# A two-layer transformer kernel: how attention scores are laid out and ordered on TensorE

## The reference, cut to what matters

```
# layer 0: causal attention inside a batch
dots = einsum('bhid,bhjd->bhij', q, k) * dh**-0.5;  dots = where(causal, -inf, dots)
out  = einsum('bhij,bhjd->bhid', softmax(dots), v)           # then top-1 of 8 experts, silu
# layer 1: self attention (no mask), then the same queries' "recursive" attention on 2 past states
attn = softmax(q @ k.T * SCALE); output = (attn @ v) @ Wo + bo
rattn = softmax(rq @ rk[p].T * SCALE) for p in (0, 1);  rctx = mean over p of rattn @ rv[p]
gate = sigmoid([output, rctx] @ Wg + bg); output = output*(1-gate) + rctx*gate   # then top-2 of 8 experts
```

## Time and profile before

| | |
|---|---|
| median of 3 runs | 1064.85 us |
| the profiled execution's own time | 1054.27 us |
| its span | 1052.3 us |
| TensorE matmul busy | 960.2 us, 91% |
| TensorE weight load busy | 639.5 us, 61% |
| VectorE busy | 788.7 us, 75% |
| ScalarE busy | 591.6 us, 56% |
| GpSimd busy | 228.7 us, 22% |
| mean granted TensorE clock | 0.956 of full |

### The profile page before, as it was taken

The page is one execution under the profiler, slowest core; times in us unless marked ns, Lnnn a source line. Parts: engine busy times, 40 slices in busy tenths (PEclk is TensorE's granted clock), DMA queues, the critical chain, the costliest instruction groups (busy, mean ns, idle before and its releaser), DMA issues.

```text
span 1052.3 us, 17558 instructions
## 1 busy us (share of the span) xinstructions
PE 960.2 (91%) x5970; PEld 639.5 (61%) x5970; DVE 788.7 (75%) x2196; ACT 591.6 (56%) x1270; POOL 228.7 (22%) x360
## 2 busy tenths in 40 slices
PE   8889998888878989999999999999899887999992
PEld 7555665555668645555555555555555442999992
DVE  6888888776465698778888788978878784686673
ACT  2466565454555445767677676775567656443330
POOL 6132323263213234000000100001032112120073
PEclk8899999898989989999999999999999989999996
DMA  4334310010112111110000000000070000212132
GB/s 124 91 99 138 91 51 21 11 50 12 36 37 75 29 28 31 31 41 2 1 11 21 11 1 2 21 14 8 1 260 21 1 3 29 74 44 61 34 86 68
DMA packets 56497, 46.50 MB, mean 44 GB/s; under 512 B 6742, under 2 KB 46038, under 8 KB 56408
## 3 DMA queue, kind: packets, MB, share of 16 engines
q1 hardware_dynamic: 41960, 33.77, 11.4%
q0 software_dynamic: 3072, 6.30, 2.1%
q10 hardware_dynamic: 11376, 5.32, 1.8%
HBM read 22.55 MB, written 14.16 MB: 35 GB/s over the span
## 4 chain that ended last, share of the span: by engine, by line
PE 66%; DVE 20%; POOL 5%; issue 4%; ACT 2%; DMA 2%; DVEq 1%; SPq 0%; POOLq 0%; ACTq 0%
PE st L1346 13%; PE pv L1368 13%; PE ring L1332 12%; PE ring L1249 7%; PE ring L1469 4%; DVE ring L1653 4%; PE st L1456 3%; PE ring L1260 2%; PE ring L1299 2%; DVE M L1649 2%; PE st L1462 2%; DVE M L1656 2%; PE pv L1462 2%; POOL G L1041 1%; PE pv L1279 1%
## 5 line engine op out<-in xcount | busy, mean ns | idle before, releaser
L1123 ACT ACTIVATE Et<-st 128x512 f32<-128x512 f32 (+3 forms) x768 | 380.9, 548 | 211.9 <-PE st L1346 208.2
L1332 PE MATMUL ring<-Kbd,Qa 128*128 128x512 f32 (+3 forms) x512 | 203.3, 417 | 17.4 <-DVE M L1653 7.7
L1346 PE MATMUL st<-Qb,Kbd 128*128 128x512 f32 (+3 forms) x512 | 196.4, 399 | 4.4 <-ACT Et L1123 4.3
L1656 DVE TENSOR_REDUCE M<-ring 128x1 f32<-128x512 f32 x256 | 163.8, 683 | 38.4 <-PE ring L1332 37.0
L1649 DVE TENSOR_REDUCE M<-ring 128x2 f32<-128x512 f32 x256 | 162.9, 683 | 28.6 <-PE ring L1332 27.8
L1346 PEld LDWEIGHTS st<-Qb,Kbd 128*128 128x128 f32 x512 | 96.9, 195 | 89.6 <-ACT Et L1123 65.5
L1332 PEld LDWEIGHTS ring<-Kbd,Qa 128*128 128x128 f32 x512 | 100.6, 200 | 61.8 <-DVE M L1656 19.7
L1653 DVE CUSTOM_DVE_ANT_0 ring<-ring,maskw 128x128 f32<-128x128 f32 (+3 forms) x256 | 120.7, 510 | 20.9 <-PE ring L1332 19.5
L1368 PE MATMUL pv<-Et,Va 128*32 128x512 f32 (+3 forms) x1024 | 120.9, 533 | 0.7 <-POOL Et L984 0.7
L1332 PE MATMUL ring<-RKbd,Qa 128*128 128x512 f32 x256 | 108.2, 430 | 7.0 <-DVE M L1649 6.3
L1346 PE MATMUL st<-Qb,RKbd 128*128 128x512 f32 x256 | 105.4, 427 | 1.2 <-ACT Et L1123 1.0
(11 more groups left out here) (222 smaller groups left out, 1263.6 us busy)
## 6 DMA issues: line engine op xcount, KB each, us to landing
Kbd<-Ksb SPq DMA_DIRECT2D x116, 64.0 KB, 2.0
Yd<-Yt ACTq DMA_DIRECT2D x76, 64.0 KB, 1.5
Xs<-Xd SPq DMA_DIRECT2D x16, 256.0 KB, 3.0
L1W<-in_L1W SPq DMA_DIRECT2D x2, 2048.0 KB, 11.8
Xd<-zero SPq DMA_DIRECT2D x6, 512.0 KB, 3.5
W<-in_L0W SPq DMA_DIRECT2D x8, 258.0 KB, 3.5
W<-in_L0W SPq DMA_DIRECT2D x8, 256.0 KB, 4.2
Xd<-zero SPq DMA_DIRECT2D x4, 448.0 KB, 4.4
```

The lines of the kernel that those rows point to most:

```text
L1123: e.activation(Et[s // 2 % 4][:, j % 2, q0:512], st[s % NST][:, q0:512], ACT.Exp, scale=SCALE).then_inc(exp_done, 1)
L1332: ins = nc.tensor.matmul(bank(ph)[:, 0:n], Qa[u % 2][:, t * 128:(t + 1) * 128], kb[:, j, 0:n], start=True, stop=True)
L1346: nc.tensor.matmul(st[s % NST][:, q0:512], kb[:, j, c * 128:(c + 1) * 128], Qb[u % 2][:, q0:512], start=True, stop=True).then_inc(st_full, 1)
L1656: e.tensor_reduce(M[i][:, t, j, 0:1], bank(ph)[:, 0:n], AX.X, ALU.max).then_inc(mx_red, 1)
```

## The change

The second layer's `mx` and `st` contract over 32 rows alone: the stationary and moving operands are sliced at rows 32j..32j+31, so that the four heads lie on four row parts of the array, and the plain transposed keys (`KT`, `RKT`) serve in place of the block-diagonal ones. With that the second layer's key copies by DMA, the clearing of `Kbd[2]` and `RKbd`, and `DIRECT` for it go. The first layer's `mx` also contracts over 32 rows, from the same `Kbd`; its `st` still takes 128 rows.

The order changes: in the first layer four `mx` (j = 0..3) are issued in one step of every four; in the second two (j = 2, 3) and two steps later two (j = 0, 1). `back` issues `st` 0 and 1 in one step, `pv` of the tile before one step later, `st` 2 and 3 after one more. So in the second layer the maxima of heads 2, 3 meet `st` of heads 0, 1 in one step, and the maxima of heads 0, 1 meet `st` of heads 2, 3. Other starting steps move by one to three so that they fall between. The number of PSUM banks is unchanged.

```diff
-KPREP, QPREP, FRONT, BACK = 2, 7, 10, 34
-AFTER_MAX, FINISH, PREP = 4, 2, -24
+KPREP, QPREP, FRONT, BACK = 3, 7, 12, 36
+AFTER_MAX, AFTER_SUM, PREP = 3, 23, -23
-DIRECT = ((0, 0), (1, 0), (1, 1))
     def front(l, u, unit):
         for t in range(4):
-            for j in range(4):
-                do("mx", l, u, t, j)
-                yield
+            if l == 0:
+                for j in range(4):
+                    do("mx", l, u, t, j)
+                yield from wait(4)
+            else:
+                for j in (2, 3):
+                    do("mx", l, u, t, j)
+                yield from wait(2)
+                for j in (0, 1):
+                    do("mx", l, u, t, j)
+                yield from wait(2)
     def back(l, u, unit, starts, at):
         for c in range(4):
-            for j in range(4):
-                do("st", l, u, c, j)
-                yield
-                if c and j == 2:
-                    do("pv", l, u, c - 1)
-        yield
-        yield
+            do("st", l, u, c, 0)
+            do("st", l, u, c, 1)
+            yield
+            if c:
+                do("pv", l, u, c - 1)
+            yield
+            do("st", l, u, c, 2)
+            do("st", l, u, c, 3)
+            yield from wait(2)
         yield
         do("pv", l, u, 3)
         if ends_sum(unit):
             do("fin", l, u)
-            starts.setdefault(at + 20, []).append(normal(l, u))
+            starts.setdefault(at + (20 if (l, u) in ((0, 15), (1, 31)) else AFTER_SUM), []).append(normal(l, u))
     def leftovers():
-        for j in range(4):
-            do("zKbd", j)
-        yield
         do("zQK")
+        yield
...
-        for g in range(4):
-            for j in range(4):
-                yield from wait(2)
-                do("zRK", g, j)
...
-        RKbd = at("RKbd", [128, 4, 4, 512], F32R, fw0)
+        RKT = at("RKT", [128, 4, 512], F32R, fw0)
+        KT = [at(f"KT{i}", [128, 512], F32R, kbd0 + 2048 * i) for i in range(3)]
...
...
-                elif what == "kT" and a not in DIRECT:
+                elif what == "kT" and a[0] == 0 and a[1]:
...
-                elif what == "pastK":
-                    g, = a
-                    sp.wait_ge(*taken(ph))
-                    sp.wait_ge(z_rk, 4 * (g + 1))
-                    for j in range(4):
-                        r = slice(32 * j, 32 * j + 32)
-                        e.dma_start(RKbd[r, g, j, :].bitcast(F32), Ksb[g % 2][r, :].bitcast(F32)).then_inc(rkbd_in[g % 2], 16)
...
                 elif what == "kT":
                     l, u = a
...
+                    if l == 0:
+                        if u >= 3:
+                            act.wait_ge(*kbd_ready(u - 2))
+                        evict(ph, Ksb[u % 2][:, :])
+                    else:
+                        act.wait_ge(*keys_let_go(u))
+                        evict(ph, KT[u % 3][:, :])
                 elif what == "pastK":
                     g, = a
-                    gone = ksb_let_go(ph)
-                    act.wait_ge(gone[0], gone[1])
-                    evict(ph, Ksb[g % 2][:, :])
+                    experts_over()
+                    evict(ph, RKT[:, g, :])
...
                     n = 128 * (t + 1) if l == 0 else 512
-                    kb = RKbd[:, g] if kind == "rec" else Kbd[u % 3]
+                    r = slice(32 * j, 32 * j + 32)
                     pe.wait_ge(*taken(("qT", l, u)))
                     if kind == "rec":
+                        keys = RKT[r, g, :]
+                        pe.wait_ge(*taken(("pastK", g)))
+                    elif l == 1:
+                        keys = KT[u % 3][r, :]
                         pe.wait_ge(*taken(("kT", l, u)))
+                    else:
+                        keys = Kbd[u % 3][r, j, :]
...
-                    ins = nc.tensor.matmul(bank(ph)[:, 0:n], Qa[u % 2][:, t * 128:(t + 1) * 128], kb[:, j, 0:n],
-                                           start=True, stop=True)
-                    ins.then_inc(mx_full, 1)
+                    nc.tensor.matmul(bank(ph)[:, 0:n], Qa[u % 2][r, t * 128:(t + 1) * 128], keys[:, 0:n],
+                                     start=True, stop=True).then_inc(mx_full, 1)
                 elif what == "st":
...
-                    kb = RKbd[:, g] if kind == "rec" else Kbd[u % 3]
+                    r = slice(32 * j, 32 * j + 32) if l else slice(0, 128)
+                    keys = RKT[r, g, :] if kind == "rec" else KT[u % 3][r, :] if l else Kbd[u % 3][:, j, :]
...
-                    nc.tensor.matmul(st[s % NST][:, q0:512], kb[:, j, c * 128:(c + 1) * 128], Qb[u % 2][:, q0:512],
+                    nc.tensor.matmul(st[s % NST][:, q0:512], keys[:, c * 128:(c + 1) * 128], Qb[u % 2][r, q0:512],
                                      start=True, stop=True).then_inc(st_full, 1)
```

More of the change, by code:

```diff
@@ L379, in pipeline @@
             if u:
-                starts.setdefault(11 if (l, u) == (1, 1) else 16 * u + KPREP, []).append(kprep(l, u, unit))
+                starts.setdefault(16 * u + KPREP, []).append(kprep(l, u, unit))
                 starts.setdefault(16 * u + QPREP, []).append(qprep(l, u, unit))
@@ L691, in program, with kbd_ready, keys_let_go, last_max @@
         n_add = {ph: n for n, ph in enumerate(p for p in order if p[0] == "norm" and units[p[1]][p[2]][0] == "rec")}
[L692 to L696, removed]
+        kbd_no = [sum(v % 3 == u % 3 for v in range(1, u)) for u in range(16)]
+        L1_KEYS = [u for u, unit in enumerate(L1_UNITS) if unit[0] != "rec"]
         def earlier(ph, names, same):
             return next((p for p in order[:spot_of[ph]][::-1] if p[0] in names and same(p)), None)
[L702 to L709, removed]
+        def kbd_ready(u):
+            return kbd_in[u % 3], 64 * (kbd_no[u] + 1)
+        def keys_let_go(u):
+            had = [v for v in L1_KEYS if v < u and v % 3 == u % 3]
+            return st_full, n_st[("st", 1, had[-1], 3, 3) if had else ("st", 0, 15, 3, 3)] + 1
+        def last_max(l, u):
+            return n_mx["mx", l, u, 3, (3, 1)[l]] + 1
         def filled(ph):
@@ L726, in program @@
         kbd_in = [sem(f"kbd_in{i}") for i in range(3)]
-        rkbd_in = [sem(f"rkbd_in{i}") for i in range(2)]
         xs_in = [[sem(f"xs_in{l}{i}") for i in range(4)] for l in range(2)]
@@ L985, in _ @@
                                     channel_multiplier=-1).then_inc(cut_done, 1)
-                elif what in ("zKbd", "zQK", "zRK"):
+                elif what == "zQK":
                     pool.wait_ge(y_full, before(ph, "output"))
@@ L1074, in _ @@
                     evict(ph, modB[l][b][:, :])
-                elif what == "kT" and a in DIRECT:
-                    l, u = a
-                    if kbd_prev[l, u] is None:
-                        act.wait_ge(z_kbd, 1)
-                    else:
-                        m, v = kbd_prev[l, u]
-                        act.wait_ge(st_full, n_st["st", m, v, 3, 3] + 1)
+                elif ph == ("kT", 0, 0):
+                    act.wait_ge(z_kbd, 1)
                     act.wait_ge(misc_full, filled(ph))
@@ L1090, in _ @@
                     l, u = a
-                    gone = ksb_let_go(ph)
-                    if gone is not None:
-                        act.wait_ge(gone[0], gone[1])
-                    if l == 1 and u < 3:
-                        experts_over()
-                    evict(ph, Ksb[u % 2][:, :])
+                    if l == 0:
+                        if u >= 3:
+                            act.wait_ge(*kbd_ready(u - 2))
[3 more added lines that the diff above has]
+                        evict(ph, KT[u % 3][:, :])
                 elif what == "pastK":
                     g, = a
-                    gone = ksb_let_go(ph)
-                    act.wait_ge(gone[0], gone[1])
-                    evict(ph, Ksb[g % 2][:, :])
+                    experts_over()
+                    evict(ph, RKT[:, g, :])
                 elif what == "qT":
@@ L1104, in _ @@
                     if u >= 2:
-                        act.wait_ge(mx_full, n_mx["mx", l, u - 2, 3, 3] + 1)
+                        act.wait_ge(mx_full, last_max(l, u - 2))
                     elif (l, u) == (1, 1):
@@ L1769, in _ @@
                     elif l == 1:
-                        for m, v in kbd_unit[-2:]:
-                            dve.wait_ge(kbd_in[v % 3], 64 * (kbd_no[m, v] + 1))
-                        for i in range(2):
-                            dve.wait_ge(rkbd_in[i], 128)
+                        for u in (14, 15):
+                            dve.wait_ge(*kbd_ready(u))
                     e.memset(r["sums"][:, :, 0:4], 0.0)
```

59 lines of the change are left out of this document (25 added, 34 removed).

## The result

The changed kernel takes 1077.34 us (median of 4 runs, 1075.19 to 1086.25) against 1064.89 before: ratio 1.0133, interval 1.0074 to 1.0193. It is slower by 1.3%, a small difference, but clear of the interval. Forecast were 1013 us and a range that ended at 1055. A second measurement, on another chip, gave 1.0137 (1.0094 to 1.018). The kernel before takes 1052 to 1068 us on the chips used, so totals are compared as ratios to it, and stages by their profiles, of which each kernel has one. Executions of one kernel differ by some per cent: ratios are from the short ones alone, but the profiles of `l0_order_128`, `l0_rows_old_order` and `all32_fill2` are of long ones, so that their stage times are upper values.

What follows compares the result with a forecast made beforehand. TensorE was taken to bound the second layer's attention, with TensorE and VectorE close in the first. The terms -52 + 4 - 3 - 1 = -52 us took 1064.85 to 1013 us, forecast range 990 to 1035, wider range 975 to 1055.

Steps and rivals of the forecast that it cites:

- What bounds the kernel now: Opening step: TensorE alone bounds the second layer's attention (97% busy); in the first layer TensorE and VectorE are near each other.
- Part 1: Second layer's attention: 32-row products overlap in packs of four, VectorE becomes the bound at 0.91 busy, stage 450 us, -52 us.
- the two heavy units: Second layer: units of 19.90 us, all of it TensorE, were to come to about 16.2 on TensorE, still their bound.
- Part 2: Granted clock, second layer: TensorE, less busy, has six more short stretches at half clock, 0.7 us each, +4 us; bounds 0, +65.
- Part 3: First layer: maxima by fours from 32 rows, overlap gain against later `pv`, -3 us; bounds -20 and +15.
- (b): Rival: relieved TensorE stays at 1.2 GHz for long stretches of the second layer; 1085 us at four tenths; chance 0.09.
- the overlap: First layer: overlapping maxima take 26 us off TensorE, net 14 after layout changes, half of it on the path: -7.
- the layout: First layer: `st` keeps the whole array, so each of 60 groups pays one more layout change of 0.20 us, 12 us.
- Part 4: Dropped key copies, clears and direct evictions: -1 us on the path at the second layer's start, bounds -3 and 0; experts 0.
- (c): Rival: products of 32 rows do not overlap, starts 0.23 us apart, second-layer units 14.4 us; 1105 us; chance 0.05.
- (a): Rival: second layer's in-order waits eat half, plain unit 12.8 to 13 us, 1040 us; sign VectorE at 85%; chance 0.12.

Runs made afterwards that it cites:

- l0_order_128: The changed kernel with the first layer's maxima from 128 rows again, still issued four at a time; ratio to before 0.9788.
- l0_rows_old_order: The first layer in its old order, one maximum and one score product in turn, but maxima from 32 rows; ratio to before 1.0601.
- all32_fill2: The kernel with all first-layer scores from 32 rows, ordered as the second layer, with key and query transposes issued twice; ratio to before 0.9894.
- l0_pairs_128: The changed kernel with the first layer from 128 rows and its maxima issued by two; 1030 to 1049 us beside 1067 of before, without an interval.
- l0_before: The changed kernel with the first layer put back wholly (rows, order, starting steps), second layer still changed; ratio 0.9669, 1019 us where before takes 1052.
- after_again: The changed kernel itself, measured a second time on another chip; ratio to before 1.0137.
- l1_old_order: Old order in both layers, first layer from 128 rows as before, second from 32 rows; 1090 to 1185 us beside 1067 of before, without an interval.

## Why the prediction was wrong

**What bounds the kernel now: right.** The second layer was bound by TensorE. After the change TensorE is still busy longer than VectorE by the profile, 414.6 and 402.0 of 467.1 us, but work added to it hardly shows any more (1.3 us cost 0.2), so that in plain units it is no longer the bound.

**Part 1: mechanism right, size two thirds.** Forecast -52, measured -35.0. The four products of a full pack start together; the Trainium skill's page "TensorE: Matmul & The Clock Gate", Part 3, gives about 4 ns from one start to the next, and the trace agrees, the fourth starts 0.01 us after the first. Plain units take 12.1 us, inside the forecast 12 to 12.8. VectorE's share is 0.86, not 0.91; TensorE's is 0.89, not under 0.85; VectorE's idle time before the maxima fell from 64 to 34.8 us, not under 30. Part of what is missing sits in the two heavy units of 19.9 us: 16.2 us forecast, 21.4 measured. They were put at TensorE's sum of work, but their projections are a chain, product, eviction, transposes, product, and every maximum waits in order behind it. At full clock such a unit takes 19.7 us (`l0_pairs_128`), so that 3.5 of the 5.2 us are the chain and 1.7 the clock:

```profile
565.70:585.40 19.70, 16.85 (x123) 9.35 (x123) 13.19 (x30) 12.32 (x24) 0.86 (x2) 1.00 0.00 1
```

In `l0_before`, where the unit takes 21.4 us at 0.92 too, its chain holds a gate projection at half clock, 3.56 us in one piece, and the maxima are read only behind it:

```profile
564.32 3.56 PE ring L1255 x16
567.88 0.49 PE ring L1244 x4
568.37 0.48 PE ring L1334 x2
568.85 1.28 DVE M L1658 x2
```

**Part 2: the step that failed, with part 3.** The clock was taken as a matter of the second layer and priced at +4 us for the kernel, and its rival (b), which ends on the side that came, was put at 0.09 and placed there too. The second layer's clock did fall, 0.98 to 0.92, but the first layer's fell from 0.94 to 0.81. The row to be read stood in the earlier trace rows: all the falls shown there were in the first layer, in units with routing, where TensorE was busy 2.87 of 5 us before the fall. What the change takes from TensorE is taken there too. In the five last units this is +12.1 us (90.3 to 102.4), by the comparison of order by four with 128 and with 32 rows. One bound of this part does not agree with itself: four tenths of the stage at half clock are +65 here and +72 in rival (b); the forecast uses neither.

**Part 3: wrong, -3 forecast, +38.3 measured.** Its terms: the overlap (-7) saves nothing that shows; VectorE waits 44.3 us for the products of the maxima, where it waited 15.8. The order by four was named (a group takes the whole ring) but not priced; it costs 15.6 us. The text had a transpose wait for the maxima, and the timeline shows the reverse: the fourth maximum waits for the transpose's eviction on ScalarE, behind exponentials, with `st` and `pv` behind it. The 32 rows cost 22.7 us. Of these the layout makes some 6 (priced at 12), an estimate from the 0.36 us that a unit in pairs loses at full clock. The clock makes most of the rest: 12.1 us in the five units at 0.67, and some of the 9.2 in the nine at 0.95. These two shares are worked out from differences of profiles, and were not each measured by itself.

**Part 4: not shown, and the experts are open.** The -1 us at the second layer's start can't be seen: its first unit takes 16.8 us at a clock of 0.50, before 15.4 at 0.70. The experts were put at 0; they lost 4.9 and 12.7 us, which is most of the 21.1 that the kernel lost. Their code is the same, and with it the last stage takes from some 175.6 us at clock 0.94 (`l0_before`) to 194.1 at 0.87 (`after_again`), the stage between the layers from 113.5 to 125.8. On the chip of `after_again`, the three kernels with the first layer put back take 185.9 to 186.3 us in the last stage, about 8 less, and 115.9 to 121.6 in the one between, where it takes 120.0. So most of the scatter comes and goes with the chip or the execution. In the last stage some of the loss may go with the changed first layer; neither was shown, and the cause is open.

**Rivals.** (c) is excluded by the packs. (a) is there in kind, in the heavy units, and VectorE's 86% is near its sign; its plain unit of 12.8 to 13 us is not. (b) was right in its direction. That its total of 1085 us is near the measured 1077 is luck: it is a sum over the second layer, which got faster.

## What to carry to other kernels

When work is taken off TensorE in a stage where it is not the bound, look first at the clock column of the stretches where it has gaps: in this kernel they are the ones that tipped over, and they pay for products that nobody changed. Row parts paid where packs stood among each other in a stage bound by TensorE; mixed one by one with whole-array products each cost 0.43 us in place of 0.23. And a group that asks for every bank of a ring makes the slowest other user of the ring its releaser: asking for half brought the cost from 14.8 us to 4.2 in nine units.

## What was not expected of the hardware

TensorE busy for 39.84 of 40 us by the profile at a granted clock of 0.50, with 32-row and whole-array products in turn and a change of layout at each; in the kernel before, a stage with 485.6 of 502.1 us busy had 0.98. So here the busy share did not tell which clock is granted. Whether that comes from products that use a quarter of the rows or from the changes of layout between them was not separated; in `l1_old_order` 493.6 of 521.5 us busy had 0.86. More work made a stretch shorter: five units of 102.4 us became 92.6. And the same code at full clock takes the same time on at least three chips, 121.9 to 122.1 us for nine units: what differs between executions is where the clock falls.
